# A mixture-of-experts block on one core: the second chunk of each expert's down product in split form, the last tile plain, and router logits in four row groups

## The chip, the cores and the metric

The kernel runs on one core of one Trainium2 chip. TensorE (PE) multiplies, VectorE (DVE), ScalarE (ACT) and GpSimd (POOL) work on vectors, and SyncE (SP) issues most transfers; each has its own queue of instructions, and they meet only at semaphores. The metric is device time in microseconds (us) from one run to the next on the same inputs; lower is better. Times inside the program are given from the start of the profiled span.

## The reference

Inputs are x of 8 x 112 x 512 and a context of 8 x 375 x 128, in float32. The first half is a cross-attention with residual, the second a feed-forward block with a shared expert and eight routed ones, of which each token uses two. Cut to what matters here:

```
x = x + attention(layernorm(x), ctx)
h = layernorm(x)                              # 896 tokens x 512
scores = softmax(h @ gate_weight.T)           # 8 experts: the router's logits
topk_w, topk_idx = top_k(scores, 2)
gu  = einsum('th,efh->tef', h, gate_up)       # 2 x 352 columns per expert
act = silu(gu[..., :352]) * gu[..., 352:]
y   = einsum('tef,te,ehf->th', act, combine, down)   # 352 rows -> 512 columns
y   = y + (silu(h @ Wg) * (h @ Wu)) @ Wd      # shared expert, 704 wide
out = x + y
```

## The kernel before

All engines' programs are written out by hand, in the order in which they run; nothing is moved by a scheduler. A wait stands in front of the instruction that needs it and holds up all that follows on that engine.

**Split and plain products.** A *plain* float32 matmul runs in two passes on PE. A *split* product writes each operand as a hi part (type fp32r) and a lo part (the rest) and adds three fp32r matmuls: lo x hi, hi x lo, hi x hi. The helper product() does this. The hi part is made by ACT (helper hi, a copy, L890), the lo part by DVE (helper lo, a subtraction, L1177). The tuples FK and FSK cut 352 and 704 rows into chunks of up to 128: an expert's down product has three chunks, of 128, 128 and 96 rows.

**From attention to router.** After the attention each of the 7 groups of 128 tokens is normalised (x2n), transposed on PE (t2, L498) and split into x2T. The 896 tokens are handled as chunk 0 (4 groups, 512 columns) and chunk 1 (3 groups, 384 columns). shared_gu(j, t) is one part j of the shared expert's gate and up product for chunk t, and shared_down(j, t) the down product. logits(t) multiplies x2T with the router's weights, split, into 8 partitions of a bank: 12 matmuls. ACT copies the result to lgT, PE transposes it in 7 pieces (L774), and DVE computes top-2, ranks and slots from it. POOL then scatters the tokens to 21 tiles of 128 rows in DRAM. In between DVE adds the shared expert's products to xres (add_shared, L1373), and PE waits for that (semaphore sres) where it needs the bank again.

**Expert loop.** Tile i (0 to 20) belongs to one expert e. Its steps on PE: gate_up(i), 24 split matmuls (L813); t_x(i+1), transposes of the next tile's input (L718); down(i-1), into bank A; t_act(i), transposes of the activations (L852). On ACT: gu_hi (hi parts of the weights of tile i+1), silu, xs_hi, dn_hi, put_y(i-1), which writes y_sb, and put_actT(i). On DVE: gu_lo in four chunks, expert_act (act_e, L1478), xs_lo, dn_lo, aT_lo. POOL scatters tile i's y_sb onto the output (L487) once it is written and the scatter before it has landed (semaphore yst); there are two y_sb buffers. In down, the first chunk of 128 rows is split, the second and third are plain (L828). Before tile 0, DVE has to finish the shared expert's adds, gu_lo(0) and xs_lo(0).

**The end.** For tile 20 PE does one chunk of gate_up, then down(19), then the rest of gate_up, and then last_down, which computes two halves of 256 columns, each with the second and third chunk plain and the first split, into banks A and D.

## Time and profile before

| | |
|---|---|
| median of 3 runs | 355.11 us (354.98 to 356.39) |
| the profiled execution's own time | 355.46 us |
| its span | 353.7 us |
| granted TensorE clock, mean over the span | 0.997 of full speed |
| busy share of the span: PE, DVE, ACT, POOL | 95%, 72%, 65%, 28% |

An engine's busy share is an average over stages with different limits. From 40 to 90 us (attention) ACT's exponentials take turns with PE, from 104 to 190 us PE computes the router's logits and the shared expert while weights arrive, and from 196 to 341 us it runs the expert loop. The difference of 1.76 us between the profiled execution's time and its span lies around the program.

### The profile page before, as it was taken

What the parts mean: (1) busy time and instruction counts of PE and PEld (TensorE: products, weight loads), DVE (VectorE), ACT (ScalarE), POOL (GpSimd) and SP (SyncE); (2) the same over time, 40 slices, a digit from 0 to 9 for tenths busy, and PEclk for the clock granted to TensorE, in tenths of its full rate; (3) what the DMA queues carried; (4) which work ended last, traced back from release to release, by engine and by line L of the source; (5) the groups of instructions that cost most, each with busy time, mean ns of one, the idle gap of its engine ahead of it and who ended that gap; (6) DMA issues with size and microseconds to landing.
All of it is one profiled execution on the core that took longest, in us unless ns stands there. A gap on an engine that the chain in (4) does not pass through costs nothing.

```text
span 353.7 us, 6947 instructions
## 1 busy us (share of the span) xinstructions
PE 336.9 (95%) x2256; PEld 278.8 (79%) x2257; DVE 254.0 (72%) x465; ACT 229.8 (65%) x610; POOL 98.3 (28%) x115
## 2 busy tenths in 40 slices
PE   8999989999999998999999899999999999999991
PEld 7898876777775886989897788788878878887771
DVE  5797978999946258846487897877787778778710
ACT  4567899999963233213225588788878887888721
POOL 4233743555540000255200011122113112311131
PEclk9999999999999999999999999999999999999998
DMA  7999100000004599993599725434443444354233
GB/s 234 374 357 379 59 3 3 2 2 2 2 2 144 234 352 353 415 348 128 169 313 229 265 91 88 90 59 69 84 86 59 75 82 81 60 85 93 30 49 43
DMA packets 28667, 49.47 MB, mean 140 GB/s; under 512 B 6752, under 2 KB 11872, under 8 KB 27616
## 3 DMA queue, kind: packets, MB, share of 16 engines
q1 hardware_dynamic: 24496, 39.91, 34.6%
q0 software_dynamic: 4144, 9.23, 15.0%
q8 instruction: 13, 0.21, 0.2%
q14 instruction: 14, 0.11, 0.1%
HBM read 32.22 MB, written 16.92 MB: 139 GB/s over the span
## 4 chain that ended last, share of the span: by engine, by line
PE 64%; ACT 13%; DVE 10%; DMA 6%; issue 3%; POOL 1%; POOLq 1%; SPq 0%; ACTq 0%; DVEq 0%
PE bank L506 25%; PE bank L813 22%; PE bank L828 9%; ACT prob L935 8%; DMA w_sg<-sguT 3%; DMA out<-y_sb,dest 3%; PE bank L852 2%; PE bank L689 2%; PE bank L718 2%; ACT probT L890 2%; DVE xres L1373 1%; DVE bn L1164 1%; DVE prob L1230 1%; DVE xnT_lo L1177 1%; POOL rstd L410 1%
## 5 line engine op out<-in xcount | busy, mean ns | idle before, releaser
L1177 DVE TENSOR_TENSOR gu_parts<-w_gu,gu_parts 128x704 fp32r<-128x704 f32 x84 | 72.8, 887 | 21.5 <-ACT gu_parts L890 20.2
L890 ACT ACTIVATE gu_parts<-w_gu 128x704 fp32r x84 | 66.3, 793 | 16.3 <-PE bank L813 15.5
L487 POOL DMA_INDIRECT out<-y_sb,dest x21 | 32.9, 1569 | 145.1 <-ACT y_sb L1098 136.9
L813 PE MATMUL bank<-gu_parts,xsT_hi 128*128 128x352 f32 x336 | 69.6, 329 | 1.2 <-issue 1.2
L813 PEld LDWEIGHTS bank<-gu_parts,xsT_hi 128*128 128x128 f32 x336 | 55.3, 188 | 2.3 <-issue 2.3
L813 PE MATMUL bank<-gu_parts,xsT_lo 128*128 128x352 f32 x168 | 40.6, 323 | 0.0
L828 PE MATMUL bank<-w_dn,actT_plain 128*128 (+1 forms) x80 | 37.6, 592 | 0.0
L506 PE MATMUL bank<-x2T_hi,w_sg_lo 128*128 128x512 f32 (+1 forms) x88 | 32.2, 366 | 0.1
L506 PE MATMUL bank<-x2T_hi,w_sg_hi 128*128 128x512 f32 (+1 forms) x88 | 32.0, 363 | 0.0
L506 PE MATMUL bank<-x2T_lo,w_sg_hi 128*128 128x512 f32 (+1 forms) x88 | 31.9, 363 | 0.0
L890 ACT ACTIVATE act_s_hi<-act_s 128x512 fp32r<-128x512 f32 (+1 forms) x10 | 5.8, 578 | 36.4 <-issue 12.2
L813 PEld LDWEIGHTS bank<-gu_parts,xsT_lo 128*128 128x128 f32 x168 | 29.3, 188 | 0.0
L471 POOL DMA_INDIRECT xs_dram<-x2n,slot_i x14 | 14.2, 1014 | 38.8 <-DVE eid L1452 34.9
L828 PEld LDWEIGHTS bank<-w_dn,actT_plain 128*128 128x128 f32 (+1 forms) x80 | 15.1, 189 | 11.4 <-issue 9.6
L935 ACT ACTIVATE prob<-score,negmax 112x112 f32<-112x112 f32 x64 | 24.1, 411 | 0.0
L1098 ACT ACTIVATE y_sb<-bank,dest 128x512 f32<-128x512 f32 x20 | 13.8, 689 | 14.2 <-PE bank L828 14.2
L935 ACT ACTIVATE prob<-bank,negmax 112x112 f32<-112x112 f32 x64 | 21.8, 362 | 1.9 <-DVE negmax L1222 1.9
L1373 DVE TENSOR_TENSOR xres<-xres,bank 128x512 f32<-128x512 f32 x35 | 22.0, 678 | 0.0
L890 ACT ACTIVATE probT<-bank 112x448 f32<-112x448 f32 x32 | 16.6, 555 | 3.9 <-PE bank L689 3.9
L1478 DVE TENSOR_TENSOR act_e<-bank,silu_e 128x352 f32<-128x352 f32 x21 | 11.0, 524 | 11.0 <-ACT silu_e L1091 11.0
L506 PEld LDWEIGHTS bank<-x2T_hi,w_sg_lo 128*128 128x128 f32 x88 | 16.5, 188 | 2.8 <-issue 0.8
L402 POOL TENSOR_TENSOR prob<-prob,rrow 112x448 f32<-112x448 f32 x16 | 14.7, 930 | 12.3 <-DVE rrow L1226 12.3
(198 smaller groups left out, 775.0 us busy)
## 6 DMA issues: line engine op xcount, KB each, us to landing
w_gu<-guT SPq DMA_DIRECT2D x8, 1408.0 KB
xs_dram<-no_row SPq DMA_DIRECT2D x1, 5460.0 KB, 19.8
xs_in<-xs_dram SPq DMA_DIRECT2D x21, 256.0 KB, 2.6
w_dn<-dnT SPq DMA_DIRECT2D x8, 512.0 KB, 5.5
w_sg<-sguT SPq DMA_DIRECT2D x10, 256.0 KB
w_dn<-dnT SPq DMA_DIRECT2D x8, 192.0 KB, 5.8
w_sd<-sdnT SPq DMA_DIRECT2D x5, 256.0 KB, 5.7
out<-xres SPq DMA_DIRECT2D x1, 1280.0 KB, 5.2
```

The source lines that it names most:

```text
L402: pool.tensor_tensor(prob[r][:, :, :], prob[r][:, :, :], rrow[:, r, :].unsqueeze(2).to_broadcast([SQ, C, SQ]), ALU.mult)\
L471: pool.indirect_dma_start(out=xs_dram[:, :], out_offset=bass.IndirectOffsetOnAxis(ap=slot_i[:, k, n:n + 1], axis=0), in_=x2n[:, n, :], in_ ...
L487: pool.indirect_dma_start(out=out[:, :], out_offset=bass.IndirectOffsetOnAxis(ap=dest[:, i, 0:1], axis=0), in_=y_sb[i % 2][:, :], in_offse ...
L506: ins = pe.matmul(dst, a, b, start=start and n == 0, stop=stop and n == len(passes) - 1)
L813: ins = pe.matmul(dst[:, 0:F], xsT[x_][:, c, :], gu2[w_][:, c, f0:f0 + F], start=c == 0 and n == 0, stop=c == C - 1 and n == 2)
L828: ins = pe.matmul(A[:, :], actT_plain[0:w, k - 1, :], w_dn[0:w, bass.ds(e * DN + k * H, H)], start=False, stop=k == len(FK) - 1)
L890: act.activation(dst, src, ACT.Copy).then_inc(s[sem], 1)
L935: ins = act.activation(prob[r][:, c, :], src, ACT.Exp, bias=negmax[:, r, c:c + 1], accum_out=rowsum[:, r, c:c + 1])
L1098: act.activation(y_sb[i % 2][:, :], A[:, :], ACT.Copy, scale=dest[:, i, 1:2].bitcast(F32))\
L1177: dve.tensor_tensor(lo_, src, hi_.bitcast(F32), ALU.subtract).then_inc(s[sem], 1)
L1373: dve.tensor_tensor(xres[:, n, :], xres[:, n, :], (B, CC, D, A)[i][:, :], ALU.add)\
L1478: dve.tensor_tensor(act_e[:, :], S[1][:, 0:F], silu_e[:, :], ALU.mult).then_inc(s["eact"], 1)
```

## The change

Five things change.

1. In down(i) of tiles 0 to 19 the second chunk of 128 rows is split as well; only the third is plain. So dn_hi, dn_lo and actT_split cover two chunks. The hi part of the first chunk's weights still comes from ACT; that of the second is copied by POOL (new function dn_hi1), in POOL's queue ahead of the scatter of the tile before.
2. Tile 20 is plain throughout. Its activations are copied to act_last, two chunks by ACT and the third by DVE; last_down computes 384 columns into bank D and 128 into bank CC. All of gate_up(20) runs before down(19), 8 filling transposes go, and ACT writes y of tile 19 behind put_last_actT.
3. The logits are computed plain. Each of the four chunks of 128 features goes to a group of 32 partitions of the bank of its own (the router's weights are padded with zeros from 8 to 32 columns by a memset on POOL), once with x2T's hi part and once with its lo part. The sum over the four groups is made where PE transposed lgT before: 7 plain matmuls with sum_gate, a matrix of zeros and ones that DVE makes by a reduce of the identity.
4. The first half of shared_gu(1, 0) is cut in two: six matmuls run between logits(0) and the transposes of the last group of tokens, six behind them. ACT casts x2T of that last group ahead of act_s_hi, and DVE splits it ahead of act_s_lo.
5. Ahead of tile 0, DVE does xs_lo(0) after two chunks of gu_lo(0) instead of three, and two adds of chunk 1 instead of one before the loop.

```diff
@@ logits, TensorE
-                product((CC, D)[t][0:E, 0:WX[t]], [(both(w_gate2, every, c, every), both(x2T, every, c, XC[t]))
-                                                   for c in range(C)]).then_inc(s["lgT"], 1)
+                for part in range(2):
+                    for c in range(C):
+                        ins = pe.matmul((CC, D)[t][HD * c:HD * (c + 1), 0:WX[t]], w_gate[:, c, :],
+                                        x2T[part][:, c, XC[t]].bitcast(F32), start=part == 0, stop=part == 1)
+                ins.then_inc(s["lgT"], 1)
...
             logits(0)
+            shared_gu(1, 0, (0,), 0, 6)
...
             t2(NX - 1, B)
-            shared_gu(1, 0, (0,))
+            shared_gu(1, 0, (0,), 6)
...
             for n in range(NX):
-                ins = pe.transpose(A[:, n * E:(n + 1) * E], lgT[:, n * P:(n + 1) * P], ident[0:E, 0:E])
+                ins = pe.matmul(A[:, n * E:(n + 1) * E], lgT[:, n * P:(n + 1) * P], sum_gate[:, 0:E], start=True, stop=True)
@@ down and last_down, TensorE
-                product(A[:, :], [(both(actT_split, every, every), both(dn2, every, every))], stop=False).then_inc(s["edn_split"], 1)
+                product(A[:, :], [(both(actT_split, every, k, every), both(dn2, every, k, every)) for k in range(2)],
+                        stop=False).then_inc(s["edn_split"], 1)
                 pe.wait_ge(s["aT"], i + 1)
-                for k, (_, w) in list(enumerate(FK))[1:]:
-                    ins = pe.matmul(A[:, :], actT_plain[0:w, k - 1, :], w_dn[0:w, bass.ds(e * DN + k * H, H)],
-                                    start=False, stop=k == len(FK) - 1)
-                ins.then_inc(s["edn"], 1)
+                w = FK[2][1]
+                pe.matmul(A[:, :], actT_plain[0:w, :], w_dn[0:w, bass.ds(e * DN + 2 * H, H)],
+                          start=False, stop=True).then_inc(s["edn"], 1)
...
+                for bank_, at, width in last_parts:
+                    for n, k in enumerate((2, 0, 1)):
+                        if n == 0:
+                            pe.wait_ge(s["aT_last"], 1)
+                        else:
+                            pe.wait_ge(s["aT"], i + 1)
+                        w = FK[k][1]
+                        ins = pe.matmul(bank_[:, 0:width], act_last[0:w, k, :], w_dn[0:w, bass.ds(e * DN + (k * H + at), width)],
+                                        start=n == 0, stop=n == 2)
+                    ins.then_inc(s["edn"], 1)
...
-            gate_up(NT - 1, range(1))
+            gate_up(NT - 1)
             pe.wait_ge(s["ey"], NT - 2)
             down(NT - 2, e_last[0])
-            gate_up(NT - 1, range(1, C))
+            t_act(NT - 1)
+            fill_with_transposes(S[2], 5)
             pe.wait_ge(s["sres"], NX * ND)
-            fill_with_transposes(CC, 8)
-            t_act(NT - 1)
-            fill_with_transposes(CC, 5)
-            pe.wait_ge(s["ey"], NT - 1)
             last_down(NT - 1, e_last[1])
@@ GpSimd
+            pool.wait_ge(s["pos"], 3)
+            pool.wait_ge(s["we"], 16 * (3 * E - 2 * n_late))
+            pool.wait_ge(s["we_late"], 16 * 2 * n_late)
+            pool.wait_ge(s["sdn"], NX * ND)
+            def dn_hi1(i):
+                e = pool.value_load(eid[0:1, i:i + 1], min_val=0, max_val=E - 1)
+                if i >= 1:
+                    pool.wait_ge(s["edn_split"], i)
+                pool.tensor_copy(dn2[0][:, 1, :], w_dn[:, bass.ds(e * DN + H, H)]).then_inc(s["dn_hi1"], 1)
+
+            dn_hi1(0)
             for i in range(NT):
+                if i + 1 < NT - 1:
+                    dn_hi1(i + 1)
+                if i == 0:
+                    pool.wait_ge(s["dest"], 16)
+                    pool.wait_ge(s["ysum0"], 16 * 3)
                 pool.wait_ge(s["ey"], i + 1)
@@ VectorE, the expert stage
             def dn_lo(e, i):
-                lo(dn2, w_dn[:, bass.ds(e * DN, H)], "dn_hi", i + 1, "dn_lo", (whole, whole))
+                dve.wait_ge(s["dn_hi1"], i + 1)
+                lo(dn2, w_dn[:, bass.ds(e * DN, 2 * H)].rearrange("p (k d) -> p k d", k=2), "dn_hi", i + 1, "dn_lo",
+                   (whole, whole, whole))
...
-                lo(actT_split, S[3][:, 0:P], "aT_hi", i + 1, "aT_lo", (whole, whole))
+                lo(actT_split, as_chunks(S[3], P)[:, 0:2, :], "aT_hi", i + 1, "aT_lo", (whole, whole, whole))
```

Three places show the order. In the instruction lists the names are those of the tensors that are written and read, and each engine's list is its own queue. First TensorE's queue in the body of the expert loop, from the transposes of the next tile's input to those of the activations; before:

```order
L718 MATMUL bank<-ident_f,xs_in 128x128 x4
L506 MATMUL bank<-dn_hi,actT_split_lo 128x512
L506 MATMUL bank<-dn_lo,actT_split_hi 128x512
L506 MATMUL bank<-dn_hi,actT_split_hi 128x512
L828 ISA
L828 MATMUL bank<-w_dn,actT_plain 128x512
L828 ISA
L828 MATMUL bank<-w_dn,actT_plain 128x512
L852 MATMUL bank<-ident,act_e 128x128 x2
```

and of the change:

```order
L737 MATMUL bank<-ident_f,xs_in 128x128 x4
L524 MATMUL bank<-dn_hi,actT_split_lo 128x512
L524 MATMUL bank<-dn_lo,actT_split_hi 128x512
L524 MATMUL bank<-dn_hi,actT_split_hi 128x512
L524 MATMUL bank<-dn_hi,actT_split_lo 128x512
L524 MATMUL bank<-dn_lo,actT_split_hi 128x512
L524 MATMUL bank<-dn_hi,actT_split_hi 128x512
L854 ISA
L854 MATMUL bank<-w_dn,actT_plain 128x512
L876 MATMUL bank<-ident,act_e 128x128 x2
```

One plain matmul has gone and three split ones stand in its place. Second, VectorE's queue ahead of tile 0, from the second chunk of gu_lo(0) on; before:

```order
L1177 TENSOR_TENSOR gu_parts<-w_gu,gu_parts 128x704
L1373 TENSOR_TENSOR xres<-xres,bank 128x512
L1177 ISA
L1177 TENSOR_TENSOR gu_parts<-w_gu,gu_parts 128x704
L1373 TENSOR_TENSOR xres<-xres,bank 128x512 x2
L1177 TENSOR_TENSOR xsT_lo<-bank,xsT_hi 128x512
L1177 ISA
L1177 TENSOR_TENSOR gu_parts<-w_gu,gu_parts 128x704
L1373 TENSOR_TENSOR xres<-xres,bank 128x512
```

and of the change:

```order
L1186 TENSOR_TENSOR gu_parts<-w_gu,gu_parts 128x704
L1391 TENSOR_TENSOR xres<-xres,bank 128x512
L1186 TENSOR_TENSOR xsT_lo<-bank,xsT_hi 128x512
L1186 ISA
L1186 TENSOR_TENSOR gu_parts<-w_gu,gu_parts 128x704
L1391 TENSOR_TENSOR xres<-xres,bank 128x512
L1186 ISA
L1186 TENSOR_TENSOR gu_parts<-w_gu,gu_parts 128x704
L1391 TENSOR_TENSOR xres<-xres,bank 128x512 x3
```

xsT_lo now stands ahead of one gu_parts and two adds, and one add more stands ahead of the loop. Third, the end of ScalarE's queue, from the hi part of tile 19's weights on; before:

```order
L890 ACTIVATE dn_hi<-w_dn 128x512
L890 ACTIVATE actT_split_hi<-bank 128x128
L1121 ACTIVATE actT_plain<-bank 128x128
L1122 ACTIVATE actT_plain<-bank 96x128
L1098 ACTIVATE y_sb_128<-bank,dest 128x512
L1098 ACTIVATE y_sb_129<-bank,dest 128x512
L890 ISA
L890 ACTIVATE dn_hi<-w_dn 128x512
L1091 ACTIVATE silu_e<-bank 128x352
L1113 ACTIVATE actT_plain<-bank 128x128
```

and of the change:

```order
L911 ACTIVATE dn_hi<-w_dn 128x512
L1116 ACTIVATE y_sb_126<-bank,dest 128x512
L911 ACTIVATE actT_split_hi<-bank 128x256
L1135 ACTIVATE actT_plain<-bank 96x128
L1109 ACTIVATE silu_e<-bank 128x352
L1129 ACTIVATE act_last<-bank 128x256
L1116 ACTIVATE y_sb_127<-bank,dest 128x512
L1123 ACTIVATE y_sb_126<-bank,dest 128x384
L1123 ACTIVATE y_sb_126<-bank,dest 128x128
```

The y of tile 18 now comes ahead of tile 19's activations, and that of tile 19 behind the silu and the copy of tile 20.

## Rows read from the trace of the kernel before

**Rows 1.** The page: busy us, share of the span and instructions of each engine.

```profile
PE 336.9 (95%) x2256; PEld 278.8 (79%) x2257; DVE 254.0 (72%) x465; ACT 229.8 (65%) x610; POOL 98.3 (28%) x115
```

**Rows 2.** Timeline, PE, expert loop: start us, duration us, engine, line, instruction, count.

```profile
289.84 0.47 PE L506 MATMUL bank<-dn_hi,actT_split_lo 128*128 128x512 f32 x1
...
290.39 0.40 PE L506 MATMUL bank<-dn_hi,actT_split_hi 128*128 128x512 f32 x1
290.62 1.88 PE L828 MATMUL bank<-w_dn,actT_plain 128*128 x4
292.34 0.49 PE L852 MATMUL bank<-ident,act_e 128*128 128x128 f32 x3
292.59 0.88 PE L813 MATMUL bank<-gu_parts,xsT_hi 128*128 128x352 f32 x4
...
334.35 0.88 PE L813 MATMUL bank<-gu_parts,xsT_hi 128*128 128x352 f32 x4
```

**Rows 3.** Timeline, DVE, the same tile; in brackets the idle time before.

```profile
290.25 0.53 DVE L1478 TENSOR_TENSOR act_e<-bank,silu_e 128x352 f32<-128x352 f32 x1 [0.53 <-ACT silu_e L1091]
...
292.95 0.68 DVE L1177 TENSOR_TENSOR dn_lo<-w_dn,dn_hi 128x512 fp32r<-128x512 f32 x1
293.55 0.28 DVE L1177 TENSOR_TENSOR actT_split_lo<-bank,actT_split_hi 128x128 fp32r<-128x128 f32 x1
294.86 1.84 DVE L1177 TENSOR_TENSOR gu_parts<-w_gu,gu_parts 128x704 fp32r<-128x704 f32 x2 [1.02 <-ACT gu_parts L890]
```

**Rows 4.** Timeline, PE and ACT, logits of chunk 0 and the last transposes.

```profile
110.20 0.39 PE L506 MATMUL bank<-x2T_hi,w_gate_lo 128*8 128x512 f32 x1
...
113.67 0.63 PE L498 MATMUL bank<-ident,x2n 128*128 128x128 f32 x4 [0.54 <-DVE x2n L1170]
...
114.69 0.58 ACT L890 ACTIVATE x2T_hi<-bank 128x512 fp32r<-128x512 f32 x1
...
117.11 0.33 PE L506 MATMUL bank<-x2T_hi,w_sg_lo 128*128 128x384 f32 x1
```

**Rows 5.** Timeline, SP, ACT and PE, from shared weights to router.

```profile
121.49 1.23 SPq L279 DMA_DIRECT2D w_sg<-sguT  x2
...
126.08 1.06 ACT L890 ACTIVATE w_sg_hi<-w_sg 128x1024 fp32r<-128x1024 f32 x1 [2.03 <-DMA w_sg<-sguT]
...
135.06 0.47 PE L506 MATMUL bank<-w_sd_hi,act_s_lo 128*128 128x512 f32 x1 [1.10 <-DVE xres L1373]
```

**Rows 6.** Timeline, DVE and PE, ahead of the first gate_up.

```profile
193.37 0.88 DVE L1177 TENSOR_TENSOR gu_parts<-w_gu,gu_parts 128x704 fp32r<-128x704 f32 x1
...
195.37 0.68 DVE L1177 TENSOR_TENSOR xsT_lo<-bank,xsT_hi 128x512 fp32r<-128x512 f32 x1
...
196.16 0.88 PE L813 MATMUL bank<-gu_parts,xsT_hi 128*128 128x352 f32 x4 [1.23 <-issue]
```

**Rows 7.** Timeline, POOL, the last three scatters.

```profile
336.08 1.56 POOL L487 DMA_INDIRECT out<-y_sb,dest  x1 [6.25 <-ACT y_sb L1098]
341.52 1.56 POOL L487 DMA_INDIRECT out<-y_sb,dest  x1 [3.89 <-DMA out<-y_sb,dest]
347.35 1.56 POOL L487 DMA_INDIRECT out<-y_sb,dest  x1 [4.27 <-ACT y_sb L1106]
```

**Rows 8.** Timeline, POOL and DVE, two in the attention and one split of 1024 columns.

```profile
37.76 5.01 POOL L424 TENSOR_TENSOR w_o_lo<-w_o,w_o_hi 128x512 fp32r<-128x512 f32 x4
...
40.60 2.65 DVE L1230 TENSOR_TENSOR prob<-prob,rrow 112x448 f32<-112x448 f32 x1
...
106.35 1.22 DVE L1177 TENSOR_TENSOR w_sg_lo<-w_sg,w_sg_hi 128x1024 fp32r<-128x1024 f32 x1
```

**Rows 9.** Groups of POOL instructions by line: count, busy us, mean ns, idle before.

```profile
L420 POOL CAST w_o_hi<-w_o 128x512 fp32r<-128x512 f32 x4 | 2.3, 612 | 4.3 <-DVE w_sd_lo L1177 4.3
```

**Rows 10.** Timeline, PE, attention's product into four groups; two passes per matmul.

```profile
103.18 0.97 PE L703 MATMUL bank<-probT,v_sb 112*32 112x112 f32 x32
```

**Rows 11.** Windows, 120 to 122 us: busy by engine, clock, DMA share, GB/s.

```profile
120.00:122.00 2.00, 2.00 (x14) 1.57 (x13) 0.00 (x0) 0.49 (x1) 0.00 (x0) 1.00 0.00 0
```

More of the change, by code:

```diff
@@ L95, in loaded_and_split @@
         return raw, (m.inside(cursor, name + "_hi", shape, F32R), lo)
-    w_gate, w_gate2 = loaded_and_split(small, "w_gate", [P, C, E])
     sh = [shared_at, shared_end]
@@ L116, in build @@
     w_sd, w_sd2 = zip(*sd)
-    lgT = m.inside(small, "lgT", [E, T])
+    lgT = m.inside(small, "lgT", [P, T])
     att = [w_exp_at, shared_at]
@@ L246, in build @@
         "sg ssil sact sact_hi sact_lo sdn sres "
-        "xin Tx xs_hi xs_lo gu_hi gu_lo dn_hi dn_lo eg esil eact Ta aT_hi aT_lo aT edn_split edn ey yst").split()
+        "xin Tx xs_hi xs_lo gu_hi gu_lo dn_hi dn_hi1 dn_lo eg esil eact Ta aT_hi aT_lo aT aT_last edn_split edn ey yst").split()
     s = {n: nc.alloc_semaphore(f"s_{n}") for n in names}
@@ L427, in constants @@
             def constants():
+                pool.memset(w_gate[:, :, E:HD], 0.0).then_inc(s["wgpad"], 1)
                 own(pool.memset(tri[:, :], 1.0))
@@ L564, in scores, with shared_gu @@
                         ins.then_inc(s["S"], 1)
-            def shared_gu(j, t, halves=(0, 1)):
+            def shared_gu(j, t, halves=(0, 1), first=0, last=None):
                 k, w = FSK[j]
@@ L576, in shared_gu @@
                 if j >= 1:
-                    pe.wait_ge(s["sact"], n - NBLK + 1)
+                    pe.wait_ge(s["sact" if halves[-1] == 1 else "ssil"], n - NBLK + 1)
                 for h in halves[0:-(-2 * w // P)]:
                     ins = product(dst[h][:, 0:WX[t]], [(both(w_sg2[j % 2], every, c, slice(h * P, (h + 1) * P)),
-                                                    both(x2T, every, c, XC[t])) for c in range(C)])
+                                                    both(x2T, every, c, XC[t])) for c in range(C)],
+                                  first=first, last=last)
                 if halves[-1] == 1:
@@ L1137, in _ @@
                 if i == NT - 1:
-                    put_y(i - 1)
-                    dn_hi(e, i)
                     silu(i)
                     put_last_actT(i)
+                    put_y(i - 1)
                     break
@@ L1326, in _ @@
                 if b == 2:
-                    lo(w_gate2, w_gate[:, :, :], "wg_hi", 1, "wg_lo", (whole, whole, whole))
+                    dve.tensor_reduce(sum_gate[:, :], ident[:, :].rearrange("p (c e) -> p e c", c=C), AX.X, ALU.add)\
+                       .then_inc(s["sumg"], 1)
                 if b >= 2:
```

104 lines of the change are left out of this document (47 added, 57 removed).

## The prediction

> **What bounds the kernel now.** I read the page first, then the timeline of one tile of the expert loop, then the PE stretches where the chain of waits leaves TensorE, and last the end of the program. The reader is to see that PE is busy for 336.9 of 353.7 us [rows 1], so only two kinds of edit count: less work on PE, or a PE wait that ends earlier. The expert loop is PE's alone. From the gate_up at 292.59 to the one at 334.35 [rows 2] lie six tiles, 6.96 us each, and no PE row in between shows an idle time. Inside a tile the three split down matmuls run from 289.84 to 290.62, the last of them 0.23 us (290.39 to 290.62), and the two plain ones (four passes) from 290.62 to 292.34, 0.86 us each [rows 2]. DVE has 0.53 us idle ahead of act_e and 1.02 us ahead of the next gu_lo pair, 1.55 us per tile [rows 3]: that is all the room there is for new DVE work.
>
> Outside the loop PE waits in four places that the change touches: 0.54 us for x2n behind the logits [rows 4], 1.10 us for xres behind the router [rows 5], 1.23 us ahead of the first gate_up [rows 6], and the end, where POOL's scatters follow each other at their own pace [rows 7].
>
> **The change, part by part.**
>
> *Down of tiles 0 to 19.* One plain matmul (0.86 us) goes, three split ones come at 0.23 us, 0.69 us: 0.17 us less of PE per tile. The new ones stand in a row of six, so no further start-up is paid. Bounds: 0.22 to 0.24 us for a split gives 0.14 to 0.20 us. The last gate_up stands behind 19 of these tiles: 19 x 0.165 = 3.1 us. What has to hide for it: dn_lo grows from 128x512 (0.68 us) to 128x1024, which a DVE row of the same kind puts at 1.22 us [rows 8], 0.54 us more; aT_lo from 128 to 256 columns, about 0.14 us more as an estimate from its 0.28 us for 128 [rows 3] and 0.68 us for 512; and DVE may stand still while POOL makes its hi part. That copy is not in the trace of before; its nearest row is POOL's cast of the same size, 0.61 us [rows 9], and the far one POOL's subtract of the same size, 5.01 us for four, 1.25 us each [rows 8]. I take the cast: one input, one output. Whether the two engines hinder each other is shown once: while the four POOL subtracts ran from 37.76 to 42.77, a DVE multiply of 112x448 that started at 40.60 took 2.65 us [rows 8], and ended some 0.5 us behind the last of them; dn_lo's 512 columns take only 0.68 us, so some 2 us of that were waiting. So I charge the copy in full, once per tile: 0.54 + 0.14 + 0.61 + 0.165 (the tile is shorter) = 1.46 us against 1.55 us of idle time. It fits, by 0.1 us, and the loop stays PE's at 6.80 us. If the copy falls beside act_e or xs_lo, which read PSUM, it costs nothing. The Trainium skill says the same of the pair (SBUF — State Buffer, Who interferes with whom): a DVE instruction with two SBUF inputs and a GpSimd instruction that reads SBUF exclude each other for a whole instruction. By that rule gu_lo and the copy always exclude each other; the 2.65 us row agrees. ACT loses an instruction; its dn_hi waits for the longer split run, 0.2 us later than now, ahead of put_y which waits for PE anyway. On POOL the scatter of tile i is queued behind the copy for i+1, which starts when tile i's splits are done, before tile i's y exists: nothing is late.
>
> *Logits in four groups.* Chunk 0 now takes 12 matmuls of 0.23 us from 110.20 on, 2.8 us, then come 0.54 us of waiting and t2 at 113.67 [rows 4]. Eight plain matmuls of 512 columns one after another would take 8 x 0.86 = 6.8 us. The row nearest to them is the attention's product into four groups of 32 partitions: 16 plain matmuls of 112 columns in 0.97 us [rows 10], where one after another they would take 16 x 112/512 x 0.86 = 3.0 us, so 3.1 at a time. That gives 2.2 us; four at a time, 1.7. I take 2.0. With the six fill matmuls (6 x 0.23 = 1.4 us) PE comes to t2 at 113.6, so t2 stays where it is, and six matmuls fewer lie between it and the next chunk. The Trainium skill (TensorE: Matmul & The Clock Gate, Packing small matmuls) measured 2.38 times for three column tiles of 512 columns; by that, chunk 0 takes 2.9 us and nothing is saved there (case 5). The 0.97 us row, with four tiles of 112 columns, is better than that.
>
> Next in line is x2T of the last tile. ACT's cast starts at 114.69, behind another [rows 4]; now it comes first and starts when the transposes are done, about 0.6 us after 113.67 (four take 0.63 us there), at 114.3; plus 0.58 for it, 0.68 for DVE's subtract and 0.15 for signals, PE's next chunk starts at 115.7 instead of 117.11 [rows 4]: 1.4 us earlier. Its end lets SP load w_sg, at 121.49 now, which ACT takes at 126.08 [rows 5]. From 120 to 122 the DMA engines moved nothing [rows 11], so this load moves along with its trigger, and with it the router's chain on DVE up to xres. PE waits 1.10 us for that chain [rows 5]; PE itself gains a further 0.7 us on chunk 1 of the logits. Against that stand the 7 plain matmuls that replace 7 transposes of 0.1 us each: 14 passes of 8 columns, which the trace doesn't have; between a transpose's 0.1 us and a split matmul's 0.23 us for each pass they take 1.4 to 3.2 us. Net, PE comes to xres at worst 0.5 us late, in the middle of the bounds inside its wait. So 1.3 us is what comes out, between 0 and 1.9.
>
> *DVE's order at the first tile.* xs_lo(0) at 195.37 moves ahead of the gu_lo at 193.37 and two adds [rows 6], 2.0 us earlier. PE is then free before it: 1.23 us gained. Late next is DVE's own pile: one add more before gu_lo(1), and the longer dn_lo. I take off 0.2 us: 1.0 us, between 0.4 and 1.4.
>
> *The last tile.* Relative to the last gate_up (334.35), the last scatter starts at 13.0 now: y is ready just then, while the scatter before it would have allowed 341.52 + 5.44 = 346.96 (5.44 is the distance from 336.08 to 341.52, which waited for a landing) [rows 7]. In the new order y(19) is written behind put_last_actT. Gate_up 3.9 (a tile's 6.96 less the 2.75 from 289.84 to 292.59, less 0.3 for t_x), six splits 1.5 (0.78 + 3 x 0.23), one plain matmul 0.86, transposes until ACT sees them 0.6 (0.49 [rows 2] and a signal): 6.9; its copy of 256 columns 0.35 and y(19) with its signal 0.9 (estimates from casts of 0.58 us for 512 columns [rows 4]): scatter(19) at 8.1 (at 7.17 now); plus 5.44, scatter(20) at 13.6. The last tile's products (three plain matmuls of 384 columns and three of 128, by the 0.86 us of 512 some 2.6 us, from 7.4 on) are done by 10.9 with their copy, and no longer matter. So 0.6 us is lost, between 0 and 1.
>
> *Nothing:* the smaller edits in the attention (a cast of w_gate gone, a memset on POOL, a reduce of 128 columns on DVE); 0.2 us at most, by the 0.28 us row of 128 columns [rows 3].
>
> **The sum.** -3.1 - 1.3 - 1.0 + 0.6 = -4.8 us. The profiled execution took 355.46 us, so 350.7; the median of the runs is 0.35 us under it: 350.3 us.
>
> **Rivals.**
> 1. *DVE becomes the loop's bound, slower.* Its place is the copy against gu_lo; the price is what exceeds 1.55 us, per tile. With 1.25 us for the copy the excess is 0.54 us, the tile takes 6.80 + 0.54 = 7.34 us, 0.38 more than before, and 19 of them give +7.2 - 1.7 = +5.5: 360.6 us. It turns slower than before once the copy costs DVE 0.95 us (a tile then takes 7.05 us, 0.09 more than now, and 19 x 0.09 = 1.7 us eats the rest). For it: only 0.1 us of room. Against it: the cast's row. Chance 0.08.
> 2. *DVE binds a little.* The idle times can't be filled to the last 0.1 us, or the first tiles never catch up: 0.05 to 0.15 us per tile, 1 to 3 us: about 352.2. Chance 0.15.
> 3. *The lead at the logits is lost.* Weights or scatters decide when the router runs: 350.3 + 1.3 = 351.6. Chance 0.12. Against it: the idle DMA engines.
> 4. *The four groups don't overlap in 512 columns* (the change doesn't do what it says): 6.8 us for chunk 0 and 5.1 for chunk 1, some 6 us on the path in place of -1.3: 357.6 us. Chance 0.02, since [rows 10] has the same form.
> 5. *They overlap less in 512 columns than in 112.* At 2.4 at a time chunk 0 takes 2.9 us, t2 comes at 114.5, 0.8 us later than now: 351.1 us. Chance 0.05; the Trainium skill's 2.38 (TensorE: Matmul & The Clock Gate, Packing small matmuls) speaks for it.
> 6. *The forecast:* 350.3, chance 0.58, own range 349.2 to 351.2.
>
> **Numbers.** A measurement of this kernel can tell about 0.5%, 1.8 us. Cases 2, 3, 5 and 6 (0.90) end below 353.3 but for the far end of case 2 (0.05), and part of case 1, with a copy of 0.8 to 1.0 us, ends within the bound; so faster 0.85, same 0.06, slower 0.09. The range takes in 2, 3, 5 and 6 and the bounds of the terms (the logits term at 1.9, a tile at 0.18): 348.8 to 352.8.
>
> **What would show it.** A tile of 6.80 us with no PE idle time and dn_lo at about 1.2 us; the POOL copies at 0.6 us, and gu_lo stretched by as much in some tiles; L775's two groups at 2.0 and 1.5 us; the chunk behind them at 115.7; the first gate_up near 193.6; the last scatter 13.6 us behind the last gate_up. A DVE without idle time in the loop, or PE idle time ahead of gate_up or the splits, would prove case 1 or 2.

## The result, and the profile after

| | before | after |
|---|---|---|
| median of the runs measured together, 7 each | 356.06 us | 353.07 us |
| the profiled execution's own time | 355.46 us | 353.07 us |
| its span | 353.7 us | 351.3 us |

The ratio is 0.9928, with a 95% interval of 0.9906 to 0.9949: 0.7% faster, about half of the forecast 1.4%, and 353.07 lies above the range. In the profiled executions it is -2.4 us where the sum said -4.8. Later runs of both kernels gave 0.9903 (after_again, below).

The answer to [rows 1], from the page of the changed kernel (busy us, share, instructions of each engine):

```profile
PE 332.9 (95%) x2281; PEld 280.5 (80%) x2282; DVE 271.6 (77%) x464; ACT 230.0 (65%) x586; POOL 118.5 (34%) x136
```

PE is still the engine that is busy nearly all the time, with 4.0 us less work; DVE and POOL have taken on 18 and 20 us.

The answer to [rows 2]: the timeline of PE in one tile of the loop (start us, duration us, engine, line, instruction, count):

```profile
283.26 0.89 PE L837 MATMUL bank<-gu_parts,xsT_hi 128*128 128x352 f32 x4
...
287.23 0.45 PE L737 MATMUL bank<-ident_f,xs_in 128*128 128x128 f32 x4
287.52 0.47 PE L524 MATMUL bank<-dn_hi,actT_split_lo 128*128 128x512 f32 x1
...
288.76 0.39 PE L524 MATMUL bank<-dn_hi,actT_split_hi 128*128 128x512 f32 x1
288.99 1.02 PE L854 MATMUL bank<-w_dn,actT_plain 96*128 x2
289.85 0.49 PE L876 MATMUL bank<-ident,act_e 128*128 128x128 f32 x3
290.10 0.89 PE L837 MATMUL bank<-gu_parts,xsT_hi 128*128 128x352 f32 x4
```

The six split matmuls take 1.47 us (287.52 to 288.99), the plain one 0.86, and the tile 6.84 us. The answer to [rows 3], DVE and POOL in the same tile (idle time before in brackets):

```profile
287.92 0.52 DVE L1499 TENSOR_TENSOR act_e<-bank,silu_e 128x352 f32<-128x352 f32 x1 [0.53 <-ACT silu_e L1109]
...
289.02 2.10 DVE L1186 TENSOR_TENSOR gu_parts<-w_gu,gu_parts 128x704 fp32r<-128x704 f32 x2
...
289.33 1.04 POOL L493 CAST dn_hi<-w_dn 128x512 fp32r x1 [3.58 <-PE bank L524]
...
291.05 1.23 DVE L1186 TENSOR_TENSOR dn_lo<-w_dn,dn_hi 128x1024 fp32r<-128x1024 f32 x1
```

dn_lo takes 1.23 us, POOL's copy falls on the gu_lo pair, and of DVE's idle time 0.53 us is left, ahead of act_e. The answers to [rows 4], PE and ACT at the logits, and to [rows 5], SP, ACT and PE up to the wait for xres:

```profile
110.32 1.06 PE L775 MATMUL bank<-x2T_hi,w_gate 128*32 128x512 f32 x8
111.20 1.04 PE L775 MATMUL bank<-x2T_lo,w_gate 128*32 128x512 f32 x8
112.17 0.50 PE L524 MATMUL bank<-x2T_hi,w_sg_lo 128*128 128x512 f32 x1
...
113.70 0.63 PE L516 MATMUL bank<-ident,x2n 128*128 128x128 f32 x4
114.37 0.60 ACT L911 ACTIVATE x2T_hi<-bank 128x512 fp32r<-128x512 f32 x1 [1.46 <-PE bank L516]
115.83 0.41 PE L524 MATMUL bank<-x2T_hi,w_sg_lo 128*128 128x384 f32 x1
```

```profile
120.27 1.23 SPq L281 DMA_DIRECT2D w_sg<-sguT  x2
124.39 1.06 ACT L911 ACTIVATE w_sg_hi<-w_sg 128x1024 fp32r<-128x1024 f32 x1 [2.10 <-DMA w_sg<-sguT]
124.45 1.62 PE L798 MATMUL bank<-sum_gate,lgT 128*128 128x8 f32 x14
125.93 0.48 PE L524 MATMUL bank<-w_sd_hi,act_s_lo 128*128 128x512 f32 x1
...
133.37 0.47 PE L524 MATMUL bank<-w_sd_hi,act_s_lo 128*128 128x512 f32 x1 [0.26 <-DVE xres L1391]
```

Chunk 0 of the logits takes 1.85 us, t2 stays at its place, the next chunk starts at 115.83, and the wait for xres ends 1.7 us earlier than in [rows 5]. The answer to [rows 6] and the first two tiles behind it, DVE, PE and POOL:

```profile
192.61 0.68 DVE L1186 TENSOR_TENSOR xsT_lo<-bank,xsT_hi 128x512 fp32r<-128x512 f32 x1
...
194.00 0.81 PE L837 MATMUL bank<-gu_parts,xsT_hi 128*128 128x352 f32 x4
...
201.59 0.61 POOL L493 CAST dn_hi<-w_dn 128x512 fp32r x1 [32.00 <-issue]
202.35 1.23 DVE L1186 TENSOR_TENSOR dn_lo<-w_dn,dn_hi 128x1024 fp32r<-128x1024 f32 x1 [0.83 <-POOL dn_hi L493]
...
206.46 0.68 DVE L1186 TENSOR_TENSOR xsT_lo<-bank,xsT_hi 128x512 fp32r<-128x512 f32 x1
...
207.91 0.89 PE L837 MATMUL bank<-gu_parts,xsT_hi 128*128 128x352 f32 x4 [0.77 <-DVE xsT_lo L1186]
```

The first gate_up starts without a wait. But DVE waits 0.83 us for POOL's first copy, works off a pile until xs_lo(2), and PE pays with 0.77 us. The copy starts 2.0 us behind the last shared product (199.57), and most of these 2 us are POOL's load of the first expert's number from memory into a register, which stands in its queue behind the wait for that product (view of one source line: count, duration in ns as min/median/max, first and last start in us):

```profile
L490 POOLq TENSOR_LOAD <-eid x20: 284/287/1442, 199.7 to 325.0; - x20
```

The first load, at 199.7, is the one of 1.44 us. The answer to [rows 7], POOL's last scatters:

```profile
332.06 1.56 POOL L505 DMA_INDIRECT out<-y_sb,dest  x1 [0.64 <-ACT y_sb L1116]
339.24 1.55 POOL L505 DMA_INDIRECT out<-y_sb,dest  x1 [5.62 <-ACT y_sb L1116]
344.92 1.54 POOL L505 DMA_INDIRECT out<-y_sb,dest  x1 [4.13 <-DMA out<-y_sb,dest]
```

To compare the kernels stage by stage, this table gives the start of the first gate_up, the stretches up to gate_up(2) and gate_up(20), and the rest of the span, read from the PE timeline of each profiled execution:

| kernel | gate_up(0) | to (2) | (2) to (20) | to the end | 24 matmuls of gate_up |
|---|---|---|---|---|---|
| before | 196.16 | 12.91 | 125.28 | 19.4 | 3.89, 3.97 in turn |
| after | 194.00 | 13.91 | 123.39 | 20.0 | 3.97 |
| b_loop | 196.79 | 14.20 | 123.30 | 20.2 | 3.97 |
| b_logits | 194.01 | 12.94 | 125.28 | 19.5 | in turn |
| b_order | 194.65 | 14.29 | 125.31 | 19.3 | in turn |
| b_tail | 194.99 | 12.84 | 125.29 | 20.5 | in turn |
| b_order_sp | 194.18 | 12.92 | 125.31 | 19.5 | in turn |
| b_order_reg | 194.48 | 13.00 | 125.32 | 19.4 | in turn |
| after_again | 193.11 | 13.95 | 123.30 | 19.5 | 3.97 |
| a_early | 194.31 | 13.81 | 122.08 | 19.8 | 3.97, from tile 5 on 3.89 |
| a_early_again | 193.75 | 13.38 | 123.37 | 19.8 | 3.97 |
| a_nopool | 194.16 | 13.15 | 123.19 | 19.6 | 3.97 |
| a_yfirst | 193.53 | 13.94 | 123.30 | 19.0 | 3.97 |
| a_tail | 195.32 | 13.68 | 123.45 | 18.2 | 3.97 |
| best | 193.51 | 14.83 | 121.65 | 18.5 | 3.89 |
| best_add | 194.74 | 13.84 | 121.94 | 18.8 | 3.89 |
| best_sp | 192.19 | 13.00 | 123.31 | 18.4 | 3.97 |
| best_both | 192.74 | 12.98 | 123.26 | 18.9 | 3.97 |

The first column varies by itself: before, b_tail and b_loop are the same program up to there, and lie 1.8 us apart. The middle columns repeat within some 0.1 us where the code is the same, but for two things that the experiments turned up: a stall behind gate_up(1), and the pace of gate_up.

### The profile page after: what moved, and what is told of

Read it like the earlier page. It is cut to its first block, busy times and chain, and to the rows that moved or that the text cites. A ratio compares the mean times of both kernels' runs of the same rounds, so it can differ in the third digit from the quotient of the medians.

```text
span 351.3 us, 7091 instructions
## 1 busy us (share of the span) xinstructions
PE 332.9 (95%) x2281; PEld 280.5 (80%) x2282; DVE 271.6 (77%) x464; ACT 230.0 (65%) x586; POOL 118.5 (34%) x136
## 4 chain that ended last, share of the span: by engine, by line
PE 54%; ACT 14%; DVE 10%; DMA 9%; issue 5%; POOL 4%; SPq 1%; POOLq 1%; ACTq 0%; DVEq 0%
PE bank L837 22%; PE bank L524 19%; ACT prob L956 8%; PE bank L854 5%; POOL xs_dram L474 4%; DMA xs_dram<-x2n,slot_i 3%; DMA w_dn<-dnT 3%; PE bank L708 2%; PE bank L876 2%; ACT probT L911 2%; PE bank L737 1%; DMA out<-y_sb,dest 1%; DVE xres L1391 1%; DMA w_sg<-sguT 1%; DMA ctx<-ctxT 1%
## 5 line engine op out<-in xcount | busy, mean ns | idle before, releaser
L1186 DVE TENSOR_TENSOR gu_parts<-w_gu,gu_parts 128x704 fp32r<-128x704 f32 x84 | 78.9, 972 | 1.7 <-ACT gu_parts L911 1.6
L911 ACT ACTIVATE gu_parts<-w_gu 128x704 fp32r x84 | 66.2, 794 | 18.4 <-PE bank L837 17.2
L493 POOL CAST dn_hi<-w_dn 128x512 fp32r x20 | 19.7, 984 | 101.0 <-PE bank L524 69.0
L911 ACT ACTIVATE act_s_hi<-act_s 128x512 fp32r<-128x512 f32 (+1 forms) x10 | 5.8, 578 | 32.4 <-DVE act_s L1371 20.2
L1186 DVE TENSOR_TENSOR dn_lo<-w_dn,dn_hi 128x1024 fp32r<-128x1024 f32 x20 | 24.6, 1228 | 0.8 <-POOL dn_hi L493 0.8
L854 PE MATMUL bank<-w_dn,actT_plain 96*128 x40 | 20.5, 592 | 0.0
L404 POOL TENSOR_TENSOR prob<-prob,rrow 112x448 f32<-112x448 f32 x16 | 14.7, 931 | 11.7 <-DVE rrow L1235 11.7
```

Source lines behind the costliest of these rows:

```text
L404: pool.tensor_tensor(prob[r][:, :, :], prob[r][:, :, :], rrow[:, r, :].unsqueeze(2).to_broadcast([SQ, C, SQ]), ALU.mult)\
L493: pool.tensor_copy(dn2[0][:, 1, :], w_dn[:, bass.ds(e * DN + H, H)]).then_inc(s["dn_hi1"], 1)
L854: pe.matmul(A[:, :], actT_plain[0:w, :], w_dn[0:w, bass.ds(e * DN + 2 * H, H)], start=False, stop=True).then_inc(s["edn"], 1)
L911: act.activation(dst, src, ACT.Copy).then_inc(s[sem], 1)
L1186: dve.tensor_tensor(lo_, src, hi_.bitcast(F32), ALU.subtract).then_inc(s[sem], 1)
```

## The experiments

**One part of the change at a time, on the kernel before.** First the loop alone:

```diff
+ down: both down chunks split, dn_hi1 on POOL, dn_lo and aT_lo over two chunks (tiles 0 to 19)
  last tile, logits and the order ahead of tile 0: as before
```

> The kernel before with the split second down chunk of tiles 0 to 19 alone (POOL makes the hi part of the second chunk); the last tile, the logits and the order stay. Theory A (read from the trace of the change): a tile takes 6.84 us in place of 6.96 on average, because all gate_ups now run at the slower of the two paces that alternate in the kernel before (3.97 and 3.89 us), and some 1 us is lost to VectorE's pile in tiles 0 and 1; the time falls by 1.2 to 1.8 us. Rival B (the sum of the prediction): 6.80 us per tile, 0.2 us for the first tiles, the time falls by 2.9 us. Rival C: all of the shortfall in the first tiles comes from the other edits (an add more ahead of the loop, xs_lo early), so here tiles 0 and 1 lose nothing and the time falls by 2.2 us.

Measured: ratio 0.9981 (0.9958 to 1.0004). Theory A was right on the tile, 6.84 us. The gain is 0.7 us; its 1.2 us lie within the interval, and so does no gain at all, while rival B's 2.9 us lie outside. The first tiles cost 1.3 us (14.20 against 12.91), which settles rival C, and the end 0.9 us: there PE comes to down(19) behind a single chunk of gate_up(20), as this row of the PE timeline of b_loop shows, and the longer dn_lo isn't ready.

```profile
336.79 0.47 PE L522 MATMUL bank<-dn_hi,actT_split_lo 128*128 128x512 f32 x1 [1.30 <-DVE dn_lo L1193]
```

The logits alone:

```diff
+ logits in four row groups; shared_gu(1, 0) cut in two; x2T's last cast and split first
```

> The kernel before with the logits in four row groups, the cut shared_gu(1, 0) and the new order of casts behind it, alone. Theory A: the router's end comes 1.7 us earlier, but before the first gate_up the shared stage gives some of it back (shared weights and down weights arrive later than wanted): the first gate_up is 0.8 us earlier, and so is the end. Rival B (prediction): 1.3 us earlier. Rival C: nothing is left at the end (within 0.2 us), since VectorE's pile ahead of tile 0 sets the first gate_up.

Measured: 0.9960 (0.9941 to 0.9980), 1.4 us, with an interval from 0.7 to 2.1 us. The prediction's 1.3 fits, and so does theory A's 0.8; rival C falls.

The order on DVE alone:

```diff
-            for c in range(C - 1):
+            for c in range(C):
+                if c == 2:
+                    xs_lo(0)
                 gu_lo(e, 0, c)
...
-            add_shared(ND - 1, 1, 0, 1)
+            add_shared(ND - 1, 1, 0, 2)
```

> The kernel before with xs_lo(0) ahead of the third gu_lo(0) and two adds of chunk 1 ahead of the loop, alone. Theory A: the first gate_up is 1.3 us earlier, and with 1.5 us of idle time per tile VectorE catches up, so the end is 1.0 to 1.3 us earlier. Rival: the gain is eaten in tiles 0 and 1, where VectorE is late with gu_lo or xs_lo: 0.3 us or less is left.

Measured: 0.9968 (0.9945 to 0.9991), 1.1 us. But in its profile 1.4 us are lost between gate_up(0) and gate_up(2), and not on DVE. SP and PE in b_order:

```profile
197.33 0.39 SPq L360 DMA_DIRECT2D out<-xres  x1
...
199.01 0.34 SPq L324 DMA_DIRECT2D xs_in<-xs_dram  x1
...
204.67 0.53 PE L718 MATMUL bank<-ident_f,xs_in 128*128 128x128 f32 x4
...
206.21 0.47 PE L506 MATMUL bank<-dn_hi,actT_split_lo 128*128 128x512 f32 x1 [1.00 <-issue]
```

The load of tile 2's input is issued 1.7 us behind the 1280 KB of the sum, since PE is earlier and the sum is not. In the kernel before, the same two rows of SP are 3.1 us apart:

```profile
197.48 0.39 SPq L360 DMA_DIRECT2D out<-xres  x1
...
200.60 0.34 SPq L324 DMA_DIRECT2D xs_in<-xs_dram  x1
```

The load lands 5.6 us after its issue, at 204.63, and the transposes start at 204.67. Behind them PE stands still for 1.00 us with no data missing. What its queue has there, behind the wait for the input, is the load of the first expert's number into a register; it starts at 204.8 and takes 0.84 us, where the median of these loads is 0.3 us:

```profile
L818 PEldq TENSOR_LOAD <-eid x21: 297/305/840, 204.8 to 333.3; - x21
```

The last tile alone:

```diff
+ act_last, last_down plain in 384 and 128 columns, gate_up(20) whole ahead of down(19),
+ y(19) behind put_last_actT; tile 19 and the loop as before
```

> The kernel before with the plain last tile alone (act_last, last_down in one piece of 384 and one of 128 columns, y of tile 19 behind the activations of tile 20; the loop stays, so tile 19 has one split chunk). Theory A: the last gate_up starts where it did, the last scatter 0.6 us later, since it follows its predecessor by 5.4 us and y(19) is written later: the time rises by 0.6 us. Rival: the scatters' landings change with their distance and the time rises by nothing or falls.

Measured: 1.0015 (0.9997 to 1.0034), 0.5 us slower, near the expected 0.6, though the interval takes in no change; its profile has 20.5 us for the end against 19.4. The four single ratios add up to -0.76%, the whole change measures -0.72%, and -0.97% when run again. With some 0.4% of uncertainty on the sum, no large help or hindrance between the parts shows, and a small one can't be excluded.

**What holds the changed kernel back.** POOL's copy taken away:

```diff
-                pool.tensor_copy(dn2[0][:, 1, :], w_dn[:, bass.ds(e * DN + H, H)]).then_inc(s["dn_hi1"], 1)
...
-                hi(dn2[0][:, 0, :], w_dn[:, bass.ds(e * DN, H)], "dn_hi")
+                hi(dn2[0][:, :, :], w_dn[:, bass.ds(e * DN, 2 * H)].rearrange("p (k d) -> p k d", k=2), "dn_hi")
```

> The changed kernel, but ScalarE makes the hi part of both down chunks (128x1024 in one copy, about 1.0 us) and POOL makes none. Theory A: the pair of gu_lo goes back from 2.10 to 1.68 us and VectorE has about 0.4 us more of idle time in each tile, but the tile stays at 6.84 us, since TensorE bounds it; tiles 0 and 1 lose about 0.8 us less, because dn_lo(0) no longer waits for POOL's first copy; in all 0.5 to 0.9 us faster than the changed kernel, if y isn't late behind the longer copy on ScalarE. Rival B: contention of VectorE and POOL is what kept the tile at 6.84 instead of 6.80 us: then the tile comes to 6.80 us or less and the gain is 1.5 us. Rival C: ScalarE's longer copy delays put_y and actT_split, and the kernel is slower by 0.5 us or more.

Measured: 0.9881 (0.9838 to 0.9923). DVE and ACT in a tile of a_nopool:

```profile
288.22 1.68 DVE L1171 TENSOR_TENSOR gu_parts<-w_gu,gu_parts 128x704 fp32r<-128x704 f32 x2
288.47 1.06 ACT L896 ACTIVATE dn_hi<-w_dn 128x1024 fp32r x1 [0.22 <-PE bank L510]
```

The pair takes 1.68 us again, and the tile stays at 6.84: rival B falls, the contention costs nothing inside the loop. In the first two tiles 0.76 us come back, as theory A said. In the times a_nopool can't be told from the changed kernel: its interval takes in after_again's 0.9903.

POOL's register load ahead of its waits:

```diff
             pool.wait_ge(s["pos"], 3)
-            pool.wait_ge(s["we"], 16 * (3 * E - 2 * n_late))
...
                 e = pool.value_load(eid[0:1, i:i + 1], min_val=0, max_val=E - 1)
+                if i == 0:
+                    pool.wait_ge(s["we"], 16 * (3 * E - 2 * n_late))
...
```

> The changed kernel, with POOL's load of the first expert's number ahead of its waits instead of behind them. Theory A: POOL's first copy starts at once when the shared products are done, about 1.5 us earlier in relation to them, dn_lo(0) doesn't wait (0.83 us now), and gate_up(2) starts 0.6 to 0.8 us earlier in relation to gate_up(1); the end moves as much. Rival: VectorE's pile at tiles 0 and 1 is its own work (adds and longer subtractions), and the wait only moves to another place: 0.2 us or nothing.

Measured: 0.9874 (0.9836 to 0.9913). The copy starts earlier (200.17), but overlaps DVE and takes 2.13 us; dn_lo(0) still waits 0.61 us, and gate_up(2) comes only 0.1 us earlier. This profile doesn't decide between the two: it also has the stall of b_order, 0.66 us of PE ahead of down(0). The second profile of the same kernel, a_early_again below, has no such stall: there the copy starts at 199.58 and takes 1.36 us, dn_lo(0) doesn't wait, and gate_up(2) comes 0.5 us earlier in relation to gate_up(1) (7.36 us against 7.89), near theory A's 0.6 to 0.8.

What nobody had expected stands in the loop. PE of a_early:

```profile
282.76 0.88 PE L838 MATMUL bank<-gu_parts,xsT_hi 128*128 128x352 f32 x4
...
286.65 0.45 PE L738 MATMUL bank<-ident_f,xs_in 128*128 128x128 f32 x4
286.94 0.47 PE L525 MATMUL bank<-dn_hi,actT_split_lo 128*128 128x512 f32 x1
...
289.50 0.41 PE L838 MATMUL bank<-gu_parts,xsT_hi 128*128 128x352 f32 x1
```

The same instructions in the same loop, and gate_up takes 3.89 us in place of 3.97, the tile 6.74. So both kernels were run again:

> The changed kernel once more. Theory A: the pace of gate_up in the loop (3.97 us for 24 matmuls in the first profile) is one of two in which a run can settle, so it may read 3.89 us here, while all that stands between stays (down and transposes 2.62 us, 6.0 and 7.9 us for the first two tiles). Theory B: the pace belongs to the program, and 3.97 us is read again.

> The changed kernel with POOL's load of the expert's number ahead of its waits, once more. Its first profile read 3.89 us for gate_up from tile 7 on, all else as in the changed kernel. Theory A (one of two paces, chosen in each execution): either can come. Theory B (the pace belongs to the program): 3.89 us again, and a tile of 6.75 us.

Measured: 0.9903 (0.9871 to 0.9936) and 0.9906 (0.9876 to 0.9936); both read 3.97 us in nearly every tile. Theory B falls with a_early_again: the pace doesn't belong to the program. In all, 3 of 12 profiles of the new loop show 3.89 us for most tiles. All six of the old loop alternate; in before, b_logits, b_order and b_order_reg the even tiles take 3.89 us, in b_tail and b_order_sp the odd ones, so the pace isn't tied to one of two buffers that take turns either.

The end. First only y(19) ahead of the activations:

```diff
                     silu(i)
-                    put_last_actT(i)
                     put_y(i - 1)
+                    put_last_actT(i)
```

> The changed kernel with y of tile 19 ahead of put_last_actT on ScalarE. The chain at the end is y(19), its scatter, the landing, the last scatter; the products of tile 20 are done 3 us before they are needed. Theory A: y(19) starts when its product is seen, 0.2 us or so earlier, so the last scatter comes 0.2 to 0.4 us earlier behind the last gate_up (13.4 in place of 13.6 us). Rival: y(19) was bound by TensorE's plain product anyway and nothing moves.

Measured: 0.9860 (0.9833 to 0.9887). Scatter(19) starts 7.34 us behind gate_up(20) in place of 7.95, and the last scatter 12.8 us in place of 13.6. But the last distance varies by itself: after_again has 7.95 and 13.1. So the gain at the last scatter is 0.3 to 0.9 us, and theory A's 0.2 to 0.4 is not refuted. Then down(19) inside gate_up(20):

```diff
-            gate_up(NT - 1)
+            gate_up(NT - 1, range(3))
             pe.wait_ge(s["ey"], NT - 2)
             down(NT - 2, e_last[0])
+            gate_up(NT - 1, range(3, C))
@@ ScalarE
+                    put_y(i - 1)
                     silu(i)
                     put_last_actT(i)
-                    put_y(i - 1)
```

> The changed kernel with down(19) between the third and the fourth chunk of gate_up(20) and y(19) ahead of the silu. Theory A: scatter(19) then waits for the landing of scatter(18) alone and comes 6.2 us behind the last gate_up (7.9 now), the last scatter 11.7 us behind it (13.6 now), since the plain last tile has its y at about 11 us: the end is 1.9 us earlier. Rival: TensorE waits for the lo parts of tile 19 and the products of tile 20 move back as in the kernel before, so that the last scatter waits for them: 0.5 us or less is gained.

Measured: 0.9865 (0.9838 to 0.9891). POOL in a_tail, with gate_up(20) at 332.45:

```profile
333.16 1.57 POOL L505 DMA_INDIRECT out<-y_sb,dest  x1 [0.64 <-ACT y_sb L1117]
338.85 1.55 POOL L505 DMA_INDIRECT out<-y_sb,dest  x1 [4.12 <-ACT y_sb L1117]
344.61 1.55 POOL L505 DMA_INDIRECT out<-y_sb,dest  x1 [4.22 <-ACT y_sb L1124]
```

Scatter(19) is at 6.4 us (theory A: 6.2) and the last one at 12.2 us (11.7). The stretch to the end is 18.2 us, against 20.0 in the changed kernel and 19.5 in after_again: 1.3 to 1.8 us of theory A's 1.9. The times don't tell a_tail from a_yfirst.

**A version that beats both.** a_nopool and a_tail together are the kernel best; best_add also moves the last add on DVE into tile 1:

> The changed kernel with two edits: ScalarE makes both down hi chunks (POOL none), and down(19) stands between the third and the fourth chunk of gate_up(20) with y(19) ahead of the silu. Theory A: the gains add up, 0.8 us in tiles 0 and 1 and 1.9 us in the tail, 2.5 us or so against the changed kernel. Rival: in the tail the longer copy on ScalarE delays y(18), and the scatters with it, and only 1.5 us is left.

> The kernel of the run best, with the last add of chunk 1 on VectorE moved from the end of tile 0 behind xs_lo(2) in tile 1, some 3 us later. Theory A: VectorE's pile ahead of xs_lo(2) is 0.6 us shorter, and gate_up(2) starts 6.85 us behind gate_up(1) (7.13 with ScalarE's copy, 7.9 in the changed kernel): 0.3 us faster than best. Rival: the sum's last transfer, which starts later, delays the load of tile 3 and the first scatter, and TensorE waits there: 0.5 us slower.

Measured: 0.9859 (0.9821 to 0.9897) and 0.9865 (0.9836 to 0.9894). Both show the fast pace, the 18.5 to 18.8 us end, and both lose behind gate_up(1) what b_order lost; best_add gains nothing that the times show. Against after_again, measured with them, they are by their ratios 1.6 and 1.4 us faster and not 2.5, with intervals that overlap, and the fast pace alone is worth 1.7 us of their profiles; so theory A of best, that the two gains add up, isn't shown. PE in best:

```profile
204.20 0.53 PE L723 MATMUL bank<-ident_f,xs_in 128*128 128x128 f32 x4 [0.57 <-DMA xs_in<-xs_dram]
205.77 0.47 PE L510 MATMUL bank<-dn_hi,actT_split_lo 128*128 128x512 f32 x1 [1.04 <-issue]
```

Here the transposes wait 0.57 us for the input. The last four runs go for this stall. SP's load first, on b_order and on best:

```diff
-            sp.wait_ge(s["sres"], NX * ND - XB[1] + 1)
-            start_sum(0, BLK + 1)
             sp.wait_ge(s["Tx"], 2)
             load_x(2)
+            sp.wait_ge(s["sres"], NX * ND - XB[1] + 1)
+            start_sum(0, BLK + 1)
```

> The kernel of b_order (the kernel before with xs_lo(0) early), with SyncE's load of tile 2's input ahead of the first transfer of the sum onto the output instead of behind it. Theory A: b_order lost 1.3 us between gate_up(1) and gate_up(2) because this load was issued only 1.7 us behind the sum's 1280 KB (3.1 us in the kernel before) and landed late; ahead of it, gate_up(2) comes 6.9 to 7.0 us behind gate_up(1) (8.31 in b_order). Theory B: the loss is TensorE's load of the expert's number ahead of down(0), and stays at 1 us. Theory C: VectorE's pile of adds makes it, and it stays at 1.3 us.

> The kernel of the run best (both hi chunks by ScalarE, down(19) inside gate_up(20)), with SyncE's load of tile 2's input ahead of the first transfer of the sum. Theory A: gate_up(2) comes 7.1 us or less behind gate_up(1) (8.82 in best, where TensorE waited 0.57 us for this load and 1.04 us behind it), 1.7 us faster. Theory B: 1 us of it stays. The pace of gate_up in the loop may come out at 3.89 or 3.97 us for 24 matmuls, worth up to 1.6 us over the loop whatever the edit.

and PE's register load ahead of the transposes, on b_order and on best_sp:

```diff
+            e_first = expert(0)
             t_x(2)
...
-            down(0, expert(0))
+            down(0, e_first)
```

> The kernel of b_order, with TensorE's load of the first expert's number ahead of the transposes of tile 2's input instead of behind them. Theory A (late input, and behind it a register load that can no longer run ahead): the transposes still start where they did, but the 1.00 us of issue time ahead of down(0) goes, and gate_up(2) comes 7.1 to 7.4 us behind gate_up(1). Theory B (the register load by itself): the same 7.0. Theory C (VectorE's pile): 8.3 as in b_order.

> The kernel of best_sp, with TensorE's load of the first expert's number also ahead of the transposes of tile 2's input. Theory A: nothing more to gain where the input is there in time: within 0.3 us of best_sp at gate_up(2). Theory B: 0.3 to 1 us earlier than best_sp.

Measured: b_order_sp 0.9974 (0.9956 to 0.9992), b_order_reg 0.9972 (0.9955 to 0.9988), best_sp 0.9851 (0.9827 to 0.9875), best_both 0.9847 (0.9810 to 0.9885). In the profiles the stall is gone in all four: gate_up(2) comes 6.91, 6.98, 6.98 and 6.94 us behind gate_up(1), as in the kernel before (6.98), where b_order had 8.31 and best 8.82. Theory C falls. SP and PE in best_sp:

```profile
196.94 5.25 SPq L362 DMA_DIRECT2D out<-xres  x2
...
205.19 0.88 PE L823 MATMUL bank<-gu_parts,xsT_hi 128*128 128x352 f32 x4
```

Since either edit alone removes the whole stall, a late input with the register load exposed behind it fits. The traces bear it out. In the profiles where the input landed 0.05 us or less ahead of the transposes (b_order, best, best_add) PE stood still for 1.00, 1.04 and 0.75 us, and its register load started 0.15 us behind the landing. In the changed kernel the load also starts 0.15 us behind the landing (202.70), but the transposes come only at 203.98, and nothing is lost. With the input 0.59 us ahead, in a_nopool, 0.22 us were lost. In b_order_reg it was 0.61 us ahead and the register load, now before it, started at 202.23: nothing was lost. What the edit does when the input is as late as in b_order was not measured. The times show no gain of b_order_sp over b_order, so the stall is not shown to come in most executions. best_sp is 1.5% faster than the kernel before, and best_both 1.5% too. The interval of best_sp lies below that of the change as first measured (0.9906 to 0.9949) and overlaps that of after_again (from 0.9871) by a hair.

## Why the prediction was wrong

That PE bounds the loop, and the direction, were right. The sum was 2.4 us too good. Two of its terms, the loop and the first tiles, make up 2.0 us of this; the first gate_up, 0.4 us later than forecast, makes up the rest, and is within what one profile varies.

1. *The loop term, "19 x 0.165 = 3.1 us", is where most went.* The edit itself is worth what was forecast: the stretch from t_x to the next gate_up goes from 3.03 to 2.87 us, 0.16 less (the 2.62 us in the expectation of after_again are not what the rows give). But the forecast subtracted it from the mean tile of 6.96 us, and this mean hid two kinds of tile, 6.91 and 7.01 us, with gate_up at 3.89 and 3.97 us. In the changed kernel gate_up takes 3.97 us in nearly every tile: 6.84 us, not 6.80. From gate_up(2) to gate_up(20) the gain is 1.89 us (125.28 less 123.39) where 18 x 0.165 = 2.97 was expected. Of the missing 1.08 us, 0.67 is the sum of gate_up over these 18 tiles (71.41 against 70.74 us), 0.16 stands between the last tile of the loop and gate_up(20) (7.00 against 6.84), and 0.14 is in two tiles of 6.95 and 6.87 us. This is the place of rival 2, "DVE binds a little", but not its mechanism: DVE keeps 0.53 us of idle time, and a_nopool gives DVE time back without a shorter tile. That the measured 353.07 lies within that rival's 1 to 3 us is luck, but for its other half, first tiles that come late, which is point 2.
2. *"Late next is DVE's own pile ... I take off 0.2 us" was mis-sized.* Between gate_up(0) and gate_up(2) stands one expert's down product, down(0); so the forecast is 12.91 - 0.165 + 0.2 = 12.95 us, measured 13.91, 0.96 us more. The pile contains what the prediction didn't list: POOL's first copy comes 2 us behind the last shared product, 1.44 us of it for the register load, and dn_lo(0) waits for it. a_nopool, which has no such wait, gives back 0.76 us, and a_early_again, with the load moved ahead, 0.5 us.
3. *The logits term* was right in its parts: 1.85 us for chunk 0 (forecast 2.0), t2 in place, the chunk behind at 115.83 (115.7), 1.48 us for the 14 small passes (1.4 to 3.2), 1.4 us in the times of b_logits (1.3), with 0.7 to 2.1 as its interval. Rivals 4 and 5 fell, and rival 3 with that interval.
4. *xs_lo(0) ahead* gave a first gate_up at 194.00 (193.6 forecast). Over all profiles: 195.98 on average with neither part (3), 194.44 with the order alone (3), 193.76 with both (11), so 1.5 us for this part and 0.7 for the logits on top. The logits alone have 194.01 (one profile, b_logits), 2.0 us; so the two parts may give less together than one by one, but one profile's spread of 1.8 us doesn't let that be shown.
5. *DVE and POOL* hinder each other as charged, and less: the pair of gu_lo takes 2.10 in place of 1.68 us, so the copy costs DVE 0.42 us and not 0.61. The forecast left 0.1 us of idle time per tile, and 0.53 us are left. Between 283 and 323 us DVE is busy for 36.82 of the 40 us, and for 35.19 in a_nopool, where the copy is ScalarE's. Rival 1 fell with this number. The Trainium skill's rule (SBUF — State Buffer, Who interferes with whom), that the two exclude each other for a whole instruction, agrees: the copy that starts 0.31 us into the pair takes 1.04 us and not 0.61.
6. *The last tile*: scatter(19) at 7.9 us behind gate_up(20) (8.1 forecast), the last scatter at 13.62 (13.6). The exact hit of the second is luck, since the same kernel has 13.1 in after_again. That a better place for down(19) takes off 1.3 to 1.8 us was not seen.

Why a run of the new loop settles at 3.97 and not at 3.89 us stays open. In a tile of each pace, DVE, ACT and POOL stand at the same places relative to PE to within 0.1 us, the granted clock reads 1.00 for both, and the programs differ by one line ahead of the loop or by nothing. At 3.89 us throughout, this loop's tile is 6.74 us, and the whole would have come out some 1.7 us lower (123.39 less the 121.65 of best).

## What to carry to other kernels

Before a saving per iteration is subtracted from a mean, list the iterations one by one: a mean over two kinds of tile is not a tile that exists. A stage that gets earlier drags its loads along, past transfers that have not moved; look for what now stands closer in the same queue. A new helper on a second engine can cost most where it starts, in the first iteration, where the register loads and waits ahead of it are not yet hidden. A register load whose source is ready early can stand ahead of a wait instead of behind it.
